# Six experts of hidden width 341 in 16 tiles per layer in place of 18: the remainders share four tiles

## The reference

```python
w = expert_weights(softmax(x.mean(axis=1) @ router_w.T))   # one weight for each sequence and expert, (32, 6)
h = gelu(einsum('bsd,edf->ebsf', x, W1) + b1[:, None, None, :])   # E = 6 experts, hidden width F = 341
out_e = einsum('ebsf,efd->ebsd', h, W2) + b2[:, None, None, :]
return einsum('be,ebsd->bsd', w, out_e)
```

## Time and profile before

| | before |
|---|---|
| median of 3 runs (lowest to highest) | 861.35 us (861.33 to 863.35) |
| the profiled execution, its own time | 863.21 us |
| its span, first to last instruction | 861.3 us |
| mean granted TensorE clock | 0.839 of full speed |
| busy: PE, DVE, ACT, POOL | 618.3, 630.2, 517.7, 325.4 us |

### The profile page before, as it was taken

How to read it: one execution, slowest core, us unless ns; L and a number is a source line. 1 busy time by engine, 2 the same in 40 slices (tenths; PEclk the granted TensorE clock), 3 DMA queues, 4 the chain that set the end, 5 groups by cost and what they waited for, 6 DMA issues and landing times.

```text
span 861.3 us, 11049 instructions
## 1 busy us (share of the span) xinstructions
PE 618.3 (72%) x3096; PEld 476.8 (55%) x3097; DVE 630.2 (73%) x1351; ACT 517.7 (60%) x781; POOL 325.4 (38%) x345
## 2 busy tenths in 40 slices
PE   6994752562816447298773799366999999999997
PEld 4552742561816437274552688223766766666665
DVE  1785597999999999997884121258888889887752
ACT  1587999999899898962322243243565465564432
POOL 0464110222413133140476144305456556455432
PEclk9995776877868677699675699756999999999999
DMA  5380034434455543334212366210000000000000
GB/s 173 115 302 17 0 74 79 83 70 83 83 92 104 96 82 70 70 70 132 94 30 60 97 178 173 80 34 0 2 1 10 1 10 9 1 10 10 1 10 18
DMA packets 26271, 56.48 MB, mean 66 GB/s; under 512 B 4006, under 2 KB 15375, under 8 KB 26004
## 3 DMA queue, kind: packets, MB, share of 16 engines
q0 software_dynamic: 5728, 24.56, 15.1%
q1 hardware_dynamic: 19924, 30.88, 11.8%
q10 hardware_dynamic: 576, 0.52, 0.2%
HBM read 29.89 MB, written 10.17 MB: 47 GB/s over the span
## 4 chain that ended last, share of the span: by engine, by line
PE 46%; DVE 15%; issue 13%; ACT 10%; POOL 7%; DMA 6%; POOLq 1%; ACTq 0%; SPq 0%; DVEq 0%
PE psum L1934 10%; PE psum L1675 4%; DMA s_R<-in_w 3%; PE psum L1739 3%; PE psum L1867 3%; PE psum L1740 2%; PE psum L1741 2%; DVE s_R L1200 2%; DVE s_R L1187 2%; PE psum L1964 2%; PE psum L1926 2%; POOL s_mean L656 2%; DVE s_R L1602 2%; POOL s_part L652 2%; PE psum L263 2%
## 5 line engine op out<-in xcount | busy, mean ns | idle before, releaser
L1739 PE MATMUL psum<-s_xn_lo,s_split_hi 128*128 128x368 f32 x256 | 96.3, 376 | 137.3 <-ACT s_R L889 133.8
L1739 PEld LDWEIGHTS psum<-s_xn_lo,s_split_hi 128*128 128x128 f32 x256 | 55.7, 218 | 142.0 <-ACT s_R L889 136.6
L1934 PE MATMUL psum<-s_R 128*128 128x368 f32 (+1 forms) x288 | 101.2, 477 | 4.1 <-ACT s_R L1011 4.1
L1206 DVE TENSOR_TENSOR_SCAN s_R<-s_R 128x2944 f32<-128x2944 f32 x16 | 100.7, 6291 | 0.8
L1740 PE MATMUL psum<-s_xn_hi,s_split_lo 128*128 128x368 f32 x256 | 93.2, 364 | 0.0
L1741 PE MATMUL psum<-s_xn_hi,s_split_hi 128*128 128x368 f32 x256 | 92.8, 362 | 0.0
L1011 ACT ACTIVATE s_R<-psum,s_cols 128x368 f32<-128x368 f32 x96 | 50.5, 565 | 51.9 <-PE psum L1928 51.8
L720 POOL TENSOR_TENSOR s_R<-s_R 128x368 f32<-128x368 f32 x47 | 44.9, 955 | 73.7 <-DVE s_R L1481 53.9
L750 POOL TENSOR_TENSOR s_R<-s_R 128x368 f32<-128x368 f32 x48 | 46.7, 972 | 58.1 <-DVE s_R L1602 56.5
L1934 PEld LDWEIGHTS psum<-s_R 128*128 128x128 f32 (+1 forms) x288 | 51.2, 189 | 28.6 <-issue 8.2
L896 ACT ACTIVATE s_R<-psum,s_cols 128x736 f32<-128x736 f32 x64 | 55.8, 876 | 17.6 <-PE psum L1741 12.4
(11 more groups left out here) (244 smaller groups left out, 1612.6 us busy)
## 6 DMA issues: line engine op xcount, KB each, us to landing
s_xnfm<-s_R POOLq DMA_DIRECT2D x14, 1472.0 KB, 10.5
s_R<-in_w SPq DMA_DIRECT2D x28, 256.0 KB
s_R<-in_xg SPq DMA_DIRECT2D x7, 744.0 KB, 4.1
x_sorted<-in_x_init SPq DMA_DIRECT2D x1, 5082.0 KB
s_wBC<-in_wBC SPq DMA_DIRECT2D x8, 256.0 KB, 2.7
s_R<-x_sorted SPq DMA_DIRECT2D x28, 66.0 KB, 2.5
s_R<-in_w SPq DMA_DIRECT2D x1, 1536.0 KB, 6.7
s_R<-y_rows SPq DMA_DIRECT2D x8, 184.0 KB
```

Source lines behind the costliest of these rows:

```text
L1206: dve.tensor_tensor_scan(bufB[:, u], ra[:, u], bufB[:, u], 0.0, ALU.mult, ALU.add).then_inc(ra_free, 1)
L1739: pe.matmul(bank(c), w_hi[:, s, u, k, :], xn_lo[:, a:b], start=True, stop=False)
L1934: ins = pe.matmul(bank((2, 4)[e % 2]), w, fh[0:kk, e % 3, j], start=(j == 0), stop=(j == FT - 1))
```

## The change

The six remainders of 85 hidden units, 510 in all, are laid one behind the other in four tiles of 128 (`NR = 4`, the last two rows zero), as a seventh unit `NE`. A unit of this kind can't be summed in one bank for each expert, since a tile holds rows of two experts; so its hidden values are multiplied by the expert's weight ahead of layer 2 (`weigh_rest`, on VectorE, one instruction over 4 x 368 columns), the four tiles are summed in one bank, and ACT copies the sum out (`rest_out`), for POOL to add. Each expert keeps two tiles. The weights for the rows of the four tiles are made in `expert_weights` by one more product (`wrt`) and one more reduction (`wr`). `FFN` has 32 entries, in a new order, and the slices around the attention's steps change with it.

```diff
-        FFN = ([(1, e, j) for e in (0, 1, 2) for j in range(FT)]
-               + [(2, e, j) for e in (0, 1) for j in range(FT)]
-               + [(1, e, j) for e in (3, 4) for j in range(FT)] + [(2, e, j) for e in (2, 3) for j in range(FT)]
-               + [(1, 5, 0), (1, 5, 1)] + [(2, 4, j) for j in range(FT)] + [(1, 5, 2)]
-               + [(2, 5, j) for j in range(FT)])
+               + [(1, 3, 0), (1, 3, 1)] + [(1, NE, r) for r in range(NR)]
+               + [(1, 4, 0), (1, 4, 1)] + [(2, e, j) for e in (2, 3) for j in range(FT)]
+               + [(1, 5, 0), (1, 5, 1)] + [(2, e, j) for e in (4, 5) for j in range(FT)]
+               + [(2, NE, r) for r in range(NR)])
...
+            def rest_out(f):
+                if not 0 <= f < NCH:
+                    return
+                g = f * NU + NE
+                act.wait_ge(fo_mm, g + 1)
+                act.wait_ge(facc_add, g - 1)
+                act.activation(ftmp[:, g % 2], bank((2, 4)[g % 2]), ACT.Copy).then_inc(fr_out, 1)
...
+            def weigh_rest(f):
+                if not 0 <= f < NCH:
+                    return
+                dve.wait_ge(f_free, 2 + tile_no1(f, NE, NR - 1) + 1)
+                r3 = fr.rearrange("p r (j l) -> p (r j) l", j=CB)
+                w = wr.rearrange("p r (j o) -> p (r j) o", o=1).to_broadcast([D, NR * CB, L])
+                dve.tensor_tensor(r3, r3, w, ALU.mult).then_inc(fr_weighed, 1)
...
                 step.wait()
+                step.add(dve.tensor_tensor(
+                    wrt, rmask.rearrange("p r (o e) -> p r o e", o=1).to_broadcast([D, NR, CB, NE]),
+                    ew.rearrange("p e (o b) -> p o b e", o=1).to_broadcast([D, NR, CB, NE]), ALU.mult))
                 step.add(dve.tensor_tensor(ewb, ew, b2T.rearrange("p (e o) -> p e o", o=1).to_broadcast([D, NE, CB]),
                                            ALU.mult))
                 step.wait()
+                step.add(dve.tensor_reduce(wr, wrt, AX, ALU.add))
...
                 if 0 <= f - 1:
                     expert_weights(f - 1)
+                    if not att:
+                        weigh_rest(f - 1)
                 weigh_expert(f - 1, 0)
                 weigh_expert(f - 1, 1)
...
                 if att:
                     shares_rest(c)
+                weigh_expert(f - 1, 4)
+                if att:
+                    weigh_rest(f - 1)
                 if tail:
                     split_stream(f)
...
+                            if e == NE:
+                                pe.wait_ge(fr_weighed, f + 1)
...
-                ffn(f - 1, 24, 33)
+                ffn(f - 1, 22, 26)
                 if att:
                     shares_fm(c)
-                ffn(f - 1, 33, 35)
+                ffn(f - 1, 26, 28)
                 if tail:
                     norm_transposes(pe, nF, f % 2, f, (5, 5))
...
                     if o == 0:
-                        ffn(f - 1, 35, NF)
+                        ffn(f - 1, 28, NF)
```

More of the change, by code:

```diff
@@ L35, in audio_tower @@
     FF = 341
-    FT = 3
-    FR = FF - 2 * D
+    FT = 2
+    NR = -(-NE * (FF - FT * D) // D)
+    NU = NE + 1
+    NT1 = NE * FT + NR
     K = 7
@@ L426, in audio_tower @@
         posc = take(CT, parts=K)
-        v1 = take(NE, FF)
-        v2 = take(NE, 2, D)
-        v2b = take(NE, D, parts=FR)
-        b1b = take(NE, parts=FR)
+        v1 = take(NT1, D)
+        v2 = take(NT1, D)
+        b1r = take(NR)
+        rmask = take(NR, NE)
         b2T = take(NE)
@@ L459, in audio_tower @@
         fh = take(3, FT, CT)
+        fr = take(NR, CT)
+        wr = take(NR, CB)
+        wrt = take(NR, CB, NE)
         facc = take(CT)
@@ L492, in audio_tower, with tile_no1, unit_out @@
                + [(2, e, j) for e in (0, 1) for j in range(FT)]
-               + [(1, e, j) for e in (3, 4) for j in range(FT)] + [(2, e, j) for e in (2, 3) for j in range(FT)]
-               + [(1, 5, 0), (1, 5, 1)] + [(2, 4, j) for j in range(FT)] + [(1, 5, 2)]
-               + [(2, 5, j) for j in range(FT)])
+               + [(1, 3, 0), (1, 3, 1)] + [(1, NE, r) for r in range(NR)]
+               + [(1, 4, 0), (1, 4, 1)] + [(2, e, j) for e in (2, 3) for j in range(FT)]
+               + [(1, 5, 0), (1, 5, 1)] + [(2, e, j) for e in (4, 5) for j in range(FT)]
+               + [(2, NE, r) for r in range(NR)])
+        ORDER1 = [(e, j) for layer, e, j in FFN if layer == 1]
+        def tile_no1(f, e, j):
+            return f * NT1 + ORDER1.index((e, j))
+        def unit_out(eng, f, e):
+            if e == NE:
+                eng.wait_ge(fr_out, f + 1)
+            else:
+                eng.wait_ge(fo_free, f * NE + e + 1)
         NF = len(FFN)
@@ L545, in _ @@
                 sp.dma_start(dst, t[name]).then_inc(wE_ready, 16)
-            for dst, name in ((v1, "v1"), (v2, "v2"), (v2b, "v2b"), (b1b, "b1b"), (b2T, "b2T"), (pwT, "pwT"),
+            for dst, name in ((v1, "v1"), (v2, "v2"), (b1r, "b1r"), (rmask, "rmask"), (b2T, "b2T"), (pwT, "pwT"),
                               (diag, "diag"), (ones4, "ones4")):
@@ L714, in add_expert @@
                     pool.wait_ge(fT_ready, f)
[L715 removed]
+                unit_out(pool, f, e)
                 if e:
[L717 to L718 removed]
+                    pool.wait_ge(facc_add, f * NU + e)
+                a3, t3 = (x.rearrange("p (j l) -> p j l", j=CB) for x in (facc, ftmp[:, (f * NU + e) % 2]))
                 other = bb.rearrange("p (j o) -> p j o", o=1).to_broadcast([D, CB, L]) if e == 0 else a3
@@ L1006, in gelus @@
                     if layer == 1:
-                        kk = D if j < 2 else FR
+                        i = tile_no1(f, e, j)
                         if j == 0:
-                            act.wait_ge(fo_mm, f * NE + e + 1)
-                        act.wait_ge(f_mm, (f * NE + e) * FT + j + 1)
-                        act.activation(fh[0:kk, e % 3, j], bank(j % 2 if e % 2 == 0 else (j + 1) % 2, kk), ACT.Gelu,
-                                       bias=col("b1", 2 * e + j) if j < 2 else b1b[:, e:e + 1], scale=1.0)\
-                            .then_inc(f_free, 1)
+                            if e == NE:
+                                last_read = (f - 1) * NU + NE + 1
+                            elif e < 3:
+                                last_read = (f - 1) * NU + e + 4
+                            else:
+                                last_read = f * NU + e - 2
+                            if last_read > 0:
+                                act.wait_ge(fo_mm, last_read)
+                        act.wait_ge(f_mm, i + 1)
+                        act.activation(fr[:, j] if e == NE else fh[:, e % 3, j], bank(i % 2), ACT.Gelu,
+                                       bias=b1r[:, j:j + 1] if e == NE else col("b1", 2 * e + j), scale=1.0)\
+                            .then_inc(f_free, 1)
+            def rest_out(f):
[5 more added lines that the diff above has]
+                act.activation(ftmp[:, g % 2], bank((2, 4)[g % 2]), ACT.Copy).then_inc(fr_out, 1)
             def qkv_out(c):
@@ L1044, in _ @@
                     act.activation(v1_hi[:, :, :], v1, ACT.Copy).then_inc(v1_hi_ready, 1)
-                gelus(c - 2, 18, 21)
+                gelus(c - 2, 16, 18)
                 if c < NCH:
@@ L1048, in _ @@
                     exponential(c)
-                gelus(c - 2, 27, 33)
+                gelus(c - 2, 22, 24)
                 if c < NCH:
@@ L1053, in _ @@
                     norm_copies(act, nF, (c - 1) % 2, c - 1, (5, 5), dst=xnfm, hi=xn_hi)
-                gelus(c - 1, 0, 9)
+                rest_out(c - 2)
+                gelus(c - 1, 0, 12)
                 if c + 1 < NCH:
                     norm_copies(act, nE, c % 2, c + 1, (7, 7))
-                gelus(c - 1, 15, 18)
+                gelus(c - 1, 12, 16)
             stage_end(act, 5)
@@ L1918, in ffn @@
                 for layer, e, j in FFN[lo:hi]:
-                    kk = D if j < 2 else FR
+                    n = FT * e + j
                     if layer == 1:
```

95 lines of the change are left out of this document (54 added, 41 removed).

## The result

| | before | after |
|---|---|---|
| median, 16 runs of each (lowest to highest) | 861.73 us (860.48 to 863.57) | 864.6 us (862.21 to 867.06) |
| the profiled execution, its own time | 863.21 us | 864.60 us |
| its span | 861.3 us | 862.7 us |
| mean granted TensorE clock | 0.839 | 0.836 |

The ratio is 1.0034, with a 95% interval of 1.0025 to 1.0043: the change costs 2.9 us. Two tiles per layer and chunk have gone from PE, and the kernel is no faster. Single executions of one kernel mostly lie 1 to 5 us apart (9 in one case). Part of that comes ahead of the change: in the fourteen profiled executions of this study the first softmax of the last stage ends between 574.3 and 576.9 us, though the work that was edited comes behind it. Differences between totals of under 2 to 3 us are therefore read from the turns, not from one total.

A forecast was written before the change was run, and what follows sets the result against it. PE looked like the bound, VectorE close behind; after the change VectorE's waits decide. Terms -0.2 + 6.0 + 1.1 - 2.3 = +4.6 take the profiled 863.21 us to 867.8, the median to 866.0; range 857.5 to 871.

The forecast's parts named there:

- case A: Turns with attention: VectorE's loop, with `weigh_rest` in it, gives +0.9 to +1.6 us a turn, 864 to 868; chance 0.50.
- part one: Stretch of a turn from P to `router_spread`: P + 17.3 us forecast against P + 16.22 before, +1.1.
- period: One turn, from P to the next P: 32.93 us before, 34.25 forecast, +1.3, taken as +1.2.
- `weigh_rest`: VectorE's added product of 1472 columns in part one: 1.7 us, bounds 1.6 and 1.9.
- PE's waits: PE idles 3.6 us ahead of the shares' transposes, then 1.3 us ahead of the shared tiles, for `weigh_rest`.
- P: End of the softmax's last product on VectorE in a turn, at 731.72 and 764.65 us before.
- Part two: Stretch from `router_spread` to the next P, paced by VectorE: 17.0 us forecast against 16.71, +0.25.
- pair of small instructions: `wrt` and `wr` on VectorE in part two: 0.28 us each, 0.55 in all; `wrt` meeting POOL's additions, 0.65 more.
- five periods: From P of turn 2 to P of turn 7, each at +1.2 us: +6.0.
- case D: The clock falls once a turn: 6 x 1 to 1.6 us on top of case A, 872 to 876; chance 0.12.
- The ends: Outside the five periods: up to P of turn 2 -0.2, turn 7 +1.1, turn 8 -1.5, turn 9 -0.8 us.
- Case C: PE's saving is the gain, as VectorE runs each step earlier: period 31.5 us, total about 850.5; chance 0.13.

The follow-up runs named there:

- the fill: Fourteen overwritten matmuls added in PE's idle time ahead of the shares' transposes, against the kernel after the change: 862.85 us, ratio 1.0006 to before.
- the new order: Kernel after, shared tiles' unit ahead of expert 5's in layer 2: 860.0 us with all four tiles weighed on VectorE, 846.05 with all on ScalarE.

## Why the prediction was right, and where its sizes were off

The prediction said no clear gain and rather a loss, and that came: 864.6 us against 866.0 forecast, inside the range, and 2.9 us above before where 4.6 were forecast. Its forecast case A is the mechanism: the loop over VectorE, with `weigh_rest` in it. The run with unweighed remainders and the fill shows it. Without PE's wait for `weigh_rest` part one is 1.6 us shorter and the period 1.0, as 0.55 comes back at POOL. The products of four tiles, two and one (1.68, 0.92 and 0.53 us) show it again, with part one at 17.0, 16.2 and 15.8.

That the total lies so close to the forecast is in part luck. The period was forecast at 34.1 us and measured at 33.75 where the clock held: +0.8, which is below A's own +0.9 to +1.6. With the fill, which keeps the falls of the clock out, the time was 862.85 us, and that lies below A's 864 to 868. The falls of the clock, which the sum leaves out, made up for periods forecast too long. The steps:

**`weigh_rest`:** 1.7 us forecast, 1.68 measured. PE's waits: 3.6 forecast and 2.86 measured, 1.3 and 1.32. The prediction put all of PE's gained time into the one wait ahead of the shares' transposes. But PE comes early to the scores as well and waits there for VectorE's score products: 1.4 us in four waits in one turn of the change, 0.6 in one wait before. That is the difference.

**Part one, +1.1 forecast, +0.8 measured.** The first tile of layer 1 came at P + 6.75, where 6.7 was forecast. From there to `router_spread` 10.25 us were measured and 10.6 forecast. The term that was mis-sized is the two tiles of layer 2 that left this stretch. I had priced them at 0.635 us each, by six in a row of turn 8, 1.27 together. Before, the six tiles of layer 2 here and the `spread_out` behind the first took 4.44 us from start to start, the wait of 0.47 not counted. Now four tiles with two `spread_out` take 3.16. That is 1.28 us less with one `spread_out` more, and one behind a tile of layer 1 takes some 0.35, so the two tiles were worth about 1.6.

**Part two, +0.25 forecast, nothing measured** (16.69 to 16.74 us, against 16.69 to 16.71). The pair of small instructions, with its collision and less what `first_experts` gives back, was forecast at 0.55 + 0.65 - 0.45 = 0.75 us and costs 0.45, by the run without it. The pair's own time was some 0.43 us. POOL did collide, but with the 24-column product behind `wrt` and not with `wrt` (0.97 us, so 0.8 lost, where I had 0.65). `first_experts` gave 0.55 back. The sum left out one term, at nothing: the products of experts 0 and 1 stand behind the collision too and gave back nearly 0.2.

**The last turn with attention.** I counted five periods at +1.2. Four were +0.8 (one of them with a fall of the clock on top) and the last, to P of turn 7, -0.23. There is no `first_experts` for a next chunk in it. Before, VectorE waited there for ACT (2.17 us ahead of the score products) and for PE (1.17 ahead of an expert's product), so the missing work gained nothing. Now it waits 0.20 for ACT and 1.19 for PE, and since PE has six tiles fewer on the way, part two is 15.65 us in place of 16.70. So the periods gave 3.0 us, not 6.0, without the fall. This is the largest error of the sum, and its step is that one period was taken for all five, though the last has other work.

**The clock.** The sum held nothing for it, and case D asked for a fall in every turn. Two turns of six had one in the profiled execution, for 1.34 us in turn 3 and 0.1 at most in turn 7; over the medians falls make some 1.7 us between the change with and without the fill. So D was partly true: its price for a fall (1 to 1.6) fits the one in turn 3 and is far above the one in turn 7, and the number was wrong. The Trainium skill ("TensorE: Matmul & The Clock Gate", on how HAM oscillation bites) describes a kernel in which each wait between bursts of matmuls throws the array back to its lower clock. The traces agree for some turns only, four of six in the run with unweighed remainders and two of six in the change.

**The ends.** Turn 8: -1.5 forecast, -2.0 measured; the rest: -0.8 forecast, -1.5 measured (from the last `router_spread` to the end of the span, 861.3 - 840.62 = 20.7 us before and 862.7 - 843.47 = 19.2 after). What was over-priced is `weigh_rest` ahead of experts 0 and 1, at 1.8 + 0.6 us for turn 8: the turn takes 25.1 us with four tiles on VectorE, 24.3 with two and 23.9 with one, so the whole product costs it some 1.5, an estimate from these. Turn 7 to its `router_spread`: +1.1 and +1.2.

The parts add up: P of turn 2 was 0.73 us earlier, nearly all of it ahead of the last stage, the periods +4.4 with the fall in turn 3, turn 7 +1.2, the ends -3.45, in all +1.4 us of span. That is what the two profiled executions differ by; the medians differ by 2.9 us, as the profiled execution of before was among its slower ones.

**Case C,** that PE's saving is the gain, asked for VectorE to run each step earlier. It fell for this change. As soon as VectorE had nothing of the weighing to do, in the new order, its sizes came: 31.73 us a turn (forecast for C: 31.5), and 846.05 us. Not by its sign, though. C wanted P at least 1.5 us earlier after `router_spread` than 16.71 us, and there it is 17.46; part one is 14.27 in place of 16.22. PE's 18.3 us of tiles went together with 15.5 us of gain for the kernel, once their price was not paid on the engine that paces it. How much of the 15.5 us a new order would have given the kernel before, without the change, is not shown: no run has it.

## What to carry to other kernels

Work taken from the busiest engine may be the cover of a chain on another one; ask what becomes visible once it is gone, and on which engine the new work is put. Put the price of a change on the engine whose idle time holds it: with the same order of tiles, 4.29 us on ScalarE left a gain of 15.5 us, and 1.72 us on VectorE in the loop left 1.9. Where idle time on TensorE opens, move work into it, since the idle time may cost the clock as well; and to compare variants, keep the clock equal first.
